# Multiplying s by c for two neighbouring units in one GpSimd operation, in a selective-scan and expert kernel

## The chip, the cores and the metric

The kernel runs on one core of a Trainium2 chip. The metric is the device time of one execution in microseconds (us). A core has five engines that run their own instruction streams and wait for each other at semaphores: TensorE (PE in the profile), VectorE (DVE), ScalarE (ACT), GpSimd (POOL) and SyncE (SP), which issues most of the DMA transfers. VectorE, ScalarE and TensorE's results share the eight banks of PSUM; GpSimd works on SBUF alone here.

## What is computed

The input is 32 sequences of 256 tokens with 128 features. Each token is normalised; the result is the input plus the output of a multi-head selective scan plus that of a mixture of 8 experts (top 1, with a capacity of 1024 tokens). The scan is what matters here:

```
def step(s, inp):
    d_t, u_t, B_t, C_t = inp
    dA = jnp.exp(d_t[..., None] * A)
    s = s * dA + (d_t * u_t)[..., None] * B_t[:, :, None, :]
    y_t = jnp.einsum('bhdn,bhn->bhd', s, C_t)
    return (s, y_t)
...
y = y + x * Dskip
y = y * jax.nn.silu(z)
out = y @ out_proj_w.T
```

There are 4 heads of 64 features, and 16 states n for each feature. All is in float32.

## The kernel before, in words

The 8192 tokens are cut into 16 chunks (0 to 15) of 512 tokens (two sequences). In a chunk the scan's 256 x 16 rows of state are cut into 32 units of 128 rows: unit w (0 to 31, `SLOTS`) holds 8 features with their 16 states. Units 0 to 15 are half 0, 16 to 31 half 1. All engines have a loop over w, and everything else is put into slots of this loop by hand-written tables (`STAGE_A`, `FFN`, `SOFTPLUS`, `GATE`, `GATHER`, `COMBINE`). The chunks run as: chunk 0; a loop over chunks 1 to 8, two in a pass, in which each chunk also computes one expert; a loop over chunks 9 to 14, two in a pass, in which the experts' rows are gathered back and added; chunk 15. The text calls 1 to 8 the second stage (FFN chunks) and 9 to 14 the third.

A unit goes through the engines like this:

- TensorE spreads d*u (L1182) and d (L1189) over the 128 rows into PSUM, two units ahead. The spread of d for unit w+2 waits for scan w-1; that of d*u waits for the u product before last of its bank.
- ScalarE takes the exponential of the spread d (L762).
- VectorE multiplies the spread d*u by B (L902, the u product; its order is u of unit w+1, then scan of unit w), and scans over time (L972) into `s_sb[:, w % 8, :]`, a ring of 8 buffers.
- GpSimd multiplies s by c in place (L578), `c_of[:, hf, hh, :]`, where `hh` changes every two units; it counts `p_ready`. In chunk 0 three of four of these products, in chunk 15 one of four, are made by VectorE (L979, `by_dve`), in chunks 1 to 14 none.
- TensorE sums the products of four units (a quad) over the states (L1204, `sum_quad`): quad k, units 4k to 4k+3, at w = 4k+6. The scan of unit 4k+8 overwrites the buffers and waits for that sum.

Around this, by slot w:

- TensorE and ScalarE also make the next chunk's inputs. ScalarE's silus of z and x (L675, L677, each pair between two table loads) stand at w = 9 and 19, TensorE's L1127 waits for them, and the output projection of the chunk before (L1147) stands at w = 9 and 10; VectorE's L872 adds its result at w = 11.
- VectorE, behind scan w: L860 at w = 5 and 21 (y plus D*x, one operand in PSUM), L864 at w = 6 and 22 (the gate, `g_sb` times `zs`, both in SBUF). In chunks 9 to 14 L893 at w = 14 to 21 (adds one gathered tile, `back` and `acc`, both in SBUF), the subtraction L908 (`split_low`, both in SBUF) at w = 7 and 24, and the small copy L886 at w = 0. In chunks 1 to 8 the small copy L992 at w = 16.
- GpSimd, behind product w: the scale L534 (`scale_x`, d times x) at w = 3 and 20; the memset L538 (`zero_first`) at w = 4 and 21, behind the product of its slot (the wait for the scale stands ahead of that product); in chunks 1 to 8 the subtraction L544 (`split_low`) at w = 7 and 24; in chunks 9 to 14 one indirect gather (L554) in each slot from 1 to 8. In chunk 0 it issues the 64 scatters L585.
- ScalarE rounds the result of the scale (L726, at w = 7 and 24) once the memset is done. The subtraction takes that, and its result is copied by four DMAs of SyncE (L434, `stack`) into `dsp`, which TensorE's spreads of the next half read. SyncE also loads `b_of` and `c_of` of a half (L446, `spread_bc`) once all products of the units that read the old ones are counted (`wait_products`).

Of the kernel before, what the change touches and what calls it, by code (L numbers as in the profile page):

```python
# [22 lines left out]
ALU = mybir.AluOpType  # L23
# [3 lines left out]
P = 128  # L27
# [5 lines left out]
CH = 512  # L33
CHUNKS = TOK // CH
# [4 lines left out]
UNITS = P // UC  # L39
SLOTS = HALVES * UNITS  # L40
QUADS = P // 32
U_RING, S_RING = 4, 2 * QUADS
# [44 lines left out]
def bass_mamba_moe(nc, hidden, in_w, conv_w, conv_b, xp_w, dt_w, dt_b, a_log, d_skip, out_w,  # L87
                   wg, w1, b1, w2, b2, consts, out):
    ctx = ExitStack()
    with ctx:  # L90
        def sb(name, shape, dt=F32):
            return ctx.enter_context(nc.sbuf_tensor(name, shape, dt))
# [58 lines left out]
        c_of = sb("c_of", [P, HALVES, 2, CH])  # L151
        u_sb = sb("u_sb", [P, U_RING, CH])
        s_sb = sb("s_sb", [P, S_RING, CH])
# [201 lines left out]
        def by_dve(ch, w):  # L355
            return w % QUADS < {0: HELP, CHUNKS - 1: HELP_LAST}.get(ch[0], 0)
# [148 lines left out]
        @block.gpsimd  # L505
        def _(pool):
            pool.memset(zero, 0.0).then_inc(S["zero_ready"], 1)
            pool.memset(xin, 0.0).then_inc(S["xin_zeroed"], 1)
            pool.memset(xnT[:, :, 0:TAPS - 1], 0.0).then_inc(S["xin_zeroed"], 1)
            pool.memset(weff[:, :, :], 0.0).then_inc(S["xin_zeroed"], 1)  # L510
            pool.memset(wg_sb[:, EXP:32], 0.0).then_inc(S["xin_zeroed"], 1)
            pool.memset(neg_m, -SP_M)
            pool.memset(neg_t, -SP_T)
            pool.memset(log_t1, LN_C1 - SP_M)
            pool.memset(log_t2, LN_C2 - 2 * SP_M)
            pool.memset(none, 0.0).then_inc(S["xin_zeroed"], 1)
            for b in (1, 3):
                pool.wait_ge(S["sp_chain"], 2 * b + 2)
                pool.wait_ge(S[f"x_loaded{b}"], 16)
                centre(pool, b).then_inc(S["centred_pool"], 1)  # L520
            for b in range(LN_BLK - 1):
                t = slice(b * BT, (b + 1) * BT)
                pool.wait_ge(S["rstd_ready"], b + 1)
                pool.tensor_tensor(xn[:, t, :], xn[:, t, :],
                                   rstd[:, t].unsqueeze(2).broadcast_to([P, BT, DM]),
                                   ALU.mult).then_inc(S["xn_ready"], 1)

            def scale_x(ch, hf):

                wait(pool, "stacked", per_chunk(ch, 128, 64 * hf))  # L530
                if ch == (0, None) and hf == 0:
                    pool.wait_ge(S["ein_zeroed"], 16 * EXP)
                pool.wait_ge(*tile_read(delta_in(ch, hf), f"D{hf}"))
                pool.tensor_tensor(dd[:, 1, :], dd[:, 0, :], xs_of(ch, hf), ALU.mult).then_inc(S["dx_ready"], 1)  # L534

            def zero_first():

                pool.memset(dd[:, 0, :].rearrange("p (s t) -> p s t", s=SEQS)[:, :, 0:1], 0.0  # L538
                            ).then_inc(S["dd_ready"], 1)

            def split_low(ch, hf):

                pool.wait_ge(S["hi_ready"], per_chunk(ch, 2, hf + 1))
                pool.tensor_tensor(lo, dd, hi.bitcast(F32), ALU.subtract).then_inc(S["lo_ready"], 1)  # L544

            scale_x((0, None), 0)
            pool.wait_ge(S["dx_ready"], 1)
            zero_first()
            split_low((0, None), 0)

            def gathers(tiles=range(GROUP)):

                for n in tiles:
                    pool.indirect_dma_start(back[:, n, :], None, eout[:, :],  # L554
                                            bass.IndirectOffsetOnAxis(ap=take_now[:, n:n + 1], axis=0),
                                            ).then_inc(S["back_loaded"], 16)

            def body(ch):
                for w in range(SLOTS):
                    hf, hh = w // UNITS, head_of(w)  # L560
                    if w == 1 and has_combine(ch):
                        pool.wait_ge(S["eo_free"], 16 + 32 * EXP)
                        pool.wait_ge(S["take_ready"], lin(ch, lambda c: c - FIRST_COMBINE + 1))

                    span = QUADS if ch[0] == 0 else 1
                    due = lambda what: [x for v in range(w - span + 1, w + 1) if w % span == span - 1
                                        for x in softplus_now(ch, v, what)]
                    zero_now = due("zero")
                    for of, hf_, _ in zero_now:
                        pool.wait_ge(S["dx_ready"], per_chunk(of, 2, hf_ + 1))  # L570
                    if not by_dve(ch, w):
                        if not any(by_dve(ch, v) is False for v in range(w // UNITS * UNITS, w)):
                            pool.wait_ge(*bc_loaded(ch, hf, "c"))
                        if w % UNITS == UNITS - 1 and ch[0] + 1 < CHUNKS:
                            pool.wait_ge(*tile_read(ch, f"bc{w // UNITS}"))
                        pool.wait_ge(S["scan_done"], per_chunk(ch, SLOTS, w + 1))
                        s_now = s_sb[:, w % S_RING, :]
                        pool.tensor_tensor(s_now, s_now, c_of[:, hf, hh, :], ALU.mult).then_inc(S["p_ready"], 1)  # L578
                    if zero_now:
                        zero_first()  # L580
                    if ch[0] == 0:
                        if w == 0:
                            pool.wait_ge(S["routed"], 2)
                        for i in range(w * TILES // SLOTS, (w + 1) * TILES // SLOTS):
                            pool.indirect_dma_start(ein[:, :],  # L585
                                                    bass.IndirectOffsetOnAxis(ap=put_at[:, i:i + 1], axis=0),
                                                    xn[:, i, :], None).then_inc(S["scattered"], 16)
                    for of, hf_, _ in softplus_now(ch, w, "scale"):
                        scale_x(of, hf_)
                    if low_by_pool(ch):  # L590
                        for of, hf_, _ in due("low"):
                            split_low(of, hf_)
                    if GATHER <= w < GATHER + GROUP and has_combine(ch):
                        gathers((w - GATHER,))
                    if ch[0] == CHUNKS - 1 and LAST_GATHER <= w < LAST_GATHER + GROUP:
                        if w == LAST_GATHER:
                            pool.wait_ge(S["take_ready"], TILES // GROUP)
                        gathers((w - LAST_GATHER,))

            chunks(pool, body, lambda: None)  # L600


# [705 lines left out]
```

## Time and profile before

| | |
|---|---|
| median of 3 runs | 1237.58 us (1233.49 to 1238.75) |
| profiled execution | 1234.84 us, span 1232.9 us |
| TensorE matmul busy | 1022.4 us (83%) |
| VectorE busy | 1070.5 us (87%) |
| ScalarE busy | 734.7 us (60%) |
| GpSimd busy | 858.9 us (70%) |
| products on GpSimd (L578) | 480, 628.5 us |
| mean granted TensorE clock | 0.901 of full speed |

The shares are means over the whole span. The views used below are: groups of instructions by shape, with the mean duration and the idle time before them; the waits, by who waited for whom; the chain of work that ended last, which is followed back from the last instruction; and the timeline, instruction by instruction. In the timeline a row is: start, duration, engine, line, operation, output and inputs, count, and in brackets the idle time of the engine before it with its releaser. The durations of two rows of VectorE overlap a little (a scan of 1.21 us is followed by the next operation after 1.13). A scan that ends is seen as the start of what VectorE does behind it.

### The profile page before, as it was taken

Reading aid. Unit: us, or ns where it says so; the run is one execution under the profiler, and the core shown is the slowest. Engines: PE = TensorE matmul, PEld = TensorE weight load, DVE = VectorE, ACT = ScalarE, POOL = GpSimd, SP = SyncE. Lnnn points to the kernel's source line nnn. Section 1 sums busy time; section 2 is a strip of 40 time slices with the busy share of each in tenths; the row PEclk is TensorE's granted clock in tenths of the full one; section 3 lists DMA queues with packets and bytes.
Section 4 is the critical chain, followed back from the end, with each engine's and each line's share of the span. In section 5 each row is a group of like instructions: output and inputs, shape, how many; then the busy total and the mean of one; then the engine's idle time right before and its main releaser. Section 6 shows DMA issues by size and latency. Waiting matters only on the chain.

```text
span 1232.9 us, 15308 instructions
## 1 busy us (share of the span) xinstructions
PE 1022.4 (83%) x3821; PEld 476.4 (39%) x3821; DVE 1070.5 (87%) x1331; ACT 734.7 (60%) x1117; POOL 858.9 (70%) x708
## 2 busy tenths in 40 slices
PE   0755858999999899999999997888888888888785
PEld 0522324444545454444445453333333333243322
DVE  7647968889898979899898989999898989999996
ACT  2564535767586776767685766556564756555421
POOL 2335788767676867677676769687777868686755
PEclk9988868999999999999999999788887979797765
DMA  6542325243432424342534423442434333343311
GB/s 160 157 94 68 91 79 130 57 99 69 107 80 64 103 62 111 77 94 51 119 68 98 89 57 80 86 86 48 87 71 90 81 73 68 82 85 80 72 36 34
DMA packets 81065, 103.01 MB, mean 84 GB/s; under 512 B 13280, under 2 KB 51072, under 8 KB 81024
## 3 DMA queue, kind: packets, MB, share of 16 engines
q1 hardware_dynamic: 76928, 94.18, 35.3%
q0 software_dynamic: 4096, 8.40, 2.3%
q8 instruction: 12, 0.20, 0.1%
q14 instruction: 29, 0.24, 0.1%
HBM read 18.66 MB, written 16.78 MB: 29 GB/s over the span
## 4 chain that ended last, share of the span: by engine, by line
PE 40%; DVE 24%; issue 22%; POOL 7%; ACT 3%; DVEq 1%; DMA 1%; SPq 1%; POOLq 0%; ACTq 0%
DVE u_sb L902 10%; DVE s_sb L972 8%; PE bank L1204 6%; PE bank L1171 5%; PE bank L1189 5%; PE bank L1127 4%; PE bank L1182 4%; PE bank L1114 3%; POOL expert_in L585 3%; PE bank L1135 2%; PE bank L1136 2%; PE bank L1137 2%; POOL s_sb L578 2%; PE bank L1147 2%; DVE g_sb L860 2%
## 5 line engine op out<-in xcount | busy, mean ns | idle before, releaser
L578 POOL TENSOR_TENSOR s_sb<-s_sb,c_of 128x512 f32<-128x512 f32 x480 | 628.5, 1315 | 273.2 <-DVE s_sb L972 265.1
L972 DVE TENSOR_TENSOR_SCAN s_sb<-bank,u_sb 128x512 f32<-128x512 f32 x512 | 620.4, 1212 | 0.0
L762 ACT ACTIVATE bank<-bank,a_neg 128x510 f32<-128x510 f32 x512 | 334.0, 659 | 255.9 <-PE bank L1189 246.4
L902 DVE TENSOR_TENSOR u_sb<-bank,b_of 128x512 f32<-128x512 f32 x512 | 346.2, 676 | 98.7 <-PE bank L1182 94.9
L1182 PE MATMUL bank<-dsp,sel_d 128*128 128x512 f32 x512 | 316.1, 617 | 39.8 <-DVE u_sb L902 20.4
L1189 PE MATMUL bank<-dsp,sel_d 128*128 128x512 f32 x512 | 244.5, 478 | 79.0 <-DVE s_sb L972 71.5
L1182 PEld LDWEIGHTS bank<-dsp,sel_d 128*128 128x128 f32 x512 | 104.6, 204 | 243.4 <-DVE u_sb L902 147.6
L1189 PEld LDWEIGHTS bank<-dsp,sel_d 128*128 128x128 f32 x512 | 106.5, 208 | 195.4 <-DVE s_sb L972 163.0
L1204 PE MATMUL bank<-s_sb,con 128*32 128x512 f32 x1024 | 161.2, 706 | 12.7 <-POOL s_sb L578 6.8
L1114 PE MATMUL bank<-xnT,wx 128*128 (+1 forms) x256 | 128.8, 597 | 0.0
L585 POOL DMA_INDIRECT expert_in<-xn,put_at x64 | 65.6, 1026 | 17.9 <-issue 17.8
L554 POOL DMA_INDIRECT xn<-expert_out,take_now x64 | 66.0, 1031 | 10.5 <-issue 7.4
L726 ACT ACTIVATE hi<-dd 128x1024 fp32r<-128x1024 f32 x32 | 33.9, 1058 | 61.8 <-POOL dd L538 61.8
L1127 PE MATMUL bank<-xs,bcw 128*64 128x512 f32 x64 | 46.7, 822 | 27.5 <-ACT xs L677 27.5
L1171 PE MATMUL bank<-xn 128*128 128x128 f32 x512 | 64.0, 278 | 6.4 <-ACT xn L737 6.4
L1171 PEld LDWEIGHTS bank<-xn 128*128 128x128 f32 x512 | 60.7, 191 | 17.3 <-ACT xn L737 9.9
L534 POOL TENSOR_TENSOR dd<-dd,xs 128x512 f32<-128x512 f32 x32 | 40.9, 1277 | 34.2 <-ACT dd L720 34.1
L1164 PE MATMUL bank<-xn 128*128 128x512 f32 x128 | 64.4, 605 | 0.3
L1114 PEld LDWEIGHTS bank<-xnT,wx 128*128 128x128 f32 x256 | 47.4, 189 | 27.7 <-issue 22.8
L720 ACT ACTIVATE dd<-bank,small 128x512 f32<-128x512 f32 x32 | 22.1, 690 | 52.6 <-PE bank L1138 51.6
L737 ACT ACTIVATE xn<-bank,b_now 128x512 f32<-128x512 f32 x64 | 43.1, 688 | 14.5 <-PE bank L1164 13.9
L1204 PEld LDWEIGHTS bank<-s_sb,con 128*32 128x32 f32 x1024 | 21.4, 114 | 60.0 <-issue 44.9
(140 smaller groups left out, 1045.0 us busy)
## 6 DMA issues: line engine op xcount, KB each, us to landing
b_of<-bc SPq DMA_DIRECT2D x64, 256.0 KB
c_of<-bc SPq DMA_DIRECT2D x64, 256.0 KB
dsp<-hi SPq DMA_DIRECT2D x64, 256.0 KB
dsp<-dd SPq DMA_DIRECT2D x64, 256.0 KB
expert_in<-dd SPq DMA_DIRECT2D x8, 512.0 KB, 6.4
xn<-expert_in SPq DMA_DIRECT2D x8, 512.0 KB, 5.4
xn<-L_ffn_W SPq DMA_DIRECT2D x16, 256.0 KB, 4.6
expert_out<-xn SPq DMA_DIRECT2D x16, 256.0 KB, 2.4
```

The lines of the kernel that those rows point to most:

```text
L554: pool.indirect_dma_start(back[:, n, :], None, eout[:, :], bass.IndirectOffsetOnAxis(ap=take_now[:, n:n + 1], axis=0),).then_inc(S["back_l ...
L578: pool.tensor_tensor(s_now, s_now, c_of[:, hf, hh, :], ALU.mult).then_inc(S["p_ready"], 1)
L585: pool.indirect_dma_start(ein[:, :], bass.IndirectOffsetOnAxis(ap=put_at[:, i:i + 1], axis=0), xn[:, i, :], None).then_inc(S["scattered"], 16)
L762: act.activation(d, d, ACT.Exp, scale=a_neg[:, k:k + 1]).then_inc(S["decay_ready"], 1)
L902: dve.tensor_tensor(u_sb[:, w % U_RING, :], du_ps[w % 2][:, :], b_of[:, hf, head_of(w), :], ALU.mult).then_inc(S["u_ready"], 1)
L972: dve.tensor_tensor_scan(s_sb[:, w % S_RING, :], decay_of(w)[:, :], u_sb[:, w % U_RING, :], 0.0, ALU.mult, ALU.add).then_inc(S["scan_done" ...
L1114: mm = pe.matmul(t[:, :], wx[:, hf, part, :], xnT[:, seqs, part:part + SEQ], start=(part == 0), stop=(part == TAPS - 1))
L1127: pe.matmul(t[0:4 * NS, :] if name[0] == "b" else t[:, :], w[:, hf, :], xs_of(ch, hf), start=True, stop=True).then_inc(S["misc_pe"], 1)
L1171: mm = pe.matmul(t[:, part * P:(part + 1) * P], hT[:, f, part * P:(part + 1) * P], w2_sb[:, f, :], start=(f == 0), stop=(f == FT - 1))
L1182: pe.matmul(du_ps[w % 2][:, :], sel_d[:, group_of(w), :, :].rearrange("k n d -> k (n d)"), dsp[:, hf, head_of(w), 1, :], start=True, stop= ...
L1189: pe.matmul(decay_of(w)[:, :], sel_d[:, group_of(w), :, :].rearrange("k n d -> k (n d)"), dsp[:, w // UNITS, head_of(w), 0, :], start=True ...
L1204: mm = pe.matmul(y_ps[q * 32:(q + 1) * 32, :], con[:, K_SUM + 32 * r:K_SUM + 32 * (r + 1)], s_sb[:, (QUADS * k + q) % S_RING, :], start=(r ...
```

## The change

In chunks 1 to 14 GpSimd makes the products of units w-1 and w (w odd) in one operation of 2 x 512 elements. At even w it makes none. It waits for scan w, and adds 2 to `p_ready`. The second operand is the same row of `c_of` for both units, repeated by a stride of zero (`broadcast_to`). Chunks 0 and 15 keep one product for each unit. The same lines set `span` to 2 in these chunks. `span` decides where the memset L538 (`due("zero")`) and GpSimd's subtraction L544 (`due("low")`) stand: what was due at w-1 or w is made at odd w. So the memset of w = 4 is made at w = 5, behind the pair (4,5), and the subtraction of w = 24 at w = 25, behind the pair (24,25). Those of w = 21 and 7 stay. The scales (w = 3 and 20) and the gathers (w = 1 to 8) stay in their slots.

```
-                    span = QUADS if ch[0] == 0 else 1
+                    two = 0 < ch[0] < CHUNKS - 1
+                    span = QUADS if ch[0] == 0 else 2 if two else 1
                     due = lambda what: [x for v in range(w - span + 1, w + 1) if w % span == span - 1
                                         for x in softplus_now(ch, v, what)]
...
-                    if not by_dve(ch, w):
-                        if not any(by_dve(ch, v) is False for v in range(w // UNITS * UNITS, w)):
+                    if not by_dve(ch, w) and (w % 2 or not two):
+                        if not any(by_dve(ch, v) is False for v in range(w // UNITS * UNITS, w - two)):
                             pool.wait_ge(*bc_loaded(ch, hf, "c"))
                         if w % UNITS == UNITS - 1 and ch[0] + 1 < CHUNKS:
                             pool.wait_ge(*tile_read(ch, f"bc{w // UNITS}"))
                         pool.wait_ge(S["scan_done"], per_chunk(ch, SLOTS, w + 1))
-                        s_now = s_sb[:, w % S_RING, :]
-                        pool.tensor_tensor(s_now, s_now, c_of[:, hf, hh, :], ALU.mult).then_inc(S["p_ready"], 1)
+                        n = 2 if two else 1
+                        s_now = s_sb[:, w % S_RING + 1 - n:w % S_RING + 1, :]
+                        pool.tensor_tensor(s_now, s_now, c_of[:, hf, hh, :].unsqueeze(1).broadcast_to([P, n, CH]),
+                                           ALU.mult).then_inc(S["p_ready"], n)
```

## Rows read from the trace of the kernel before

**Rows 1.** Chain that ended last, 909:977 us: start us, us, engine and line.

```profile
957.66 0.06 ACT bank L762
...
973.96 0.33 DVE acc L893
```

**Rows 2.** Waits of the whole run: who waited for whom, total us, times, longest.

```profile
ACT hi L726 <- POOL dd L538: 61.8, 32, 14.7
```

**Rows 3.** Groups by shape, GpSimd: xcount | busy us, mean ns | idle us before, releasers.

```profile
L578 POOL TENSOR_TENSOR s_sb<-s_sb,c_of 128x512 f32<-128x512 f32 x480 | 628.5, 1315 | 273.2 <-DVE s_sb L972 265.1 <-POOL dd L534 3.5 <-DMA expert_out<-xn 1.0
...
L544 POOL TENSOR_TENSOR dd<-dd,hi 128x1024 fp32r<-128x1024 f32 x17 | 40.1, 2358 | 1.2 <-ACT hi L726 1.2
...
L524 POOL TENSOR_TENSOR xn<-xn,sp_x 128x2048 f32<-128x2048 f32 x3 | 10.8, 3609 | 6.4 <-DVE sp_x L825 6.4
```

**Rows 4.** Timeline, chunk 12, units 1 to 8: start us, us, engine, operation [idle before].

```profile
946.74 1.29 POOL L578 TENSOR_TENSOR s_sb<-s_sb,c_of 128x512 f32<-128x512 f32 x1 [0.51 <-DVE s_sb L972]
...
948.18 1.00 POOL L554 DMA_INDIRECT xn<-expert_out,take_now  x1
...
956.55 0.12 POOL L538 MEMSET dd<- 128x2 f32 x1
...
956.70 1.06 ACT L726 ACTIVATE hi<-dd 128x1024 fp32r<-128x1024 f32 x1 [2.46 <-POOL dd L538]
...
958.90 1.28 ACT L675 ACT_TABLE_LOAD   x1
...
961.42 1.97 PE L1127 MATMUL bank<-xs,bcw 128*64 128x512 f32 x2 [1.49 <-ACT xs L677]
```

**Rows 5.** Timeline, chunk 4, units 4 to 11: GpSimd, ScalarE, VectorE.

```profile
406.57 0.10 POOL L538 MEMSET dd<- 128x2 f32 x1
...
406.70 1.06 ACT L726 ACTIVATE hi<-dd 128x1024 fp32r<-128x1024 f32 x1 [0.72 <-POOL dd L538]
...
410.08 1.28 ACT L675 ACT_TABLE_LOAD   x1
...
408.74 0.67 DVE L864 TENSOR_TENSOR g_sb<-g_sb,zs 128x512 f32<-128x512 f32 x1
...
417.96 0.69 DVE L872 TENSOR_TENSOR acc<-bank,acc 128x512 f32 x1
```

**Rows 6.** Timeline, chunk 15: a product and a VectorE operation beside it.

```profile
1161.99 1.28 POOL L578 TENSOR_TENSOR s_sb<-s_sb,c_of 128x512 f32<-128x512 f32 x1
...
1162.16 1.67 DVE L864 TENSOR_TENSOR g_sb<-g_sb,zs 128x512 f32<-128x512 f32 x1
```

**Rows 7.** Timeline, chunk 9: a run of products and a VectorE operation beside it.

```profile
761.92 7.44 POOL L578 TENSOR_TENSOR s_sb<-s_sb,c_of 128x512 f32<-128x512 f32 x6
...
766.44 3.07 DVE L893 SCALAR_TENSOR_TENSOR acc<-xn,gate,acc 128x128 f32 x1
```

**Rows 8.** Timeline, chunk 12, units 14 and 15: VectorE and GpSimd.

```profile
973.96 0.33 DVE L893 SCALAR_TENSOR_TENSOR acc<-xn,gate,acc 128x128 f32 x1
...
974.12 1.30 POOL L578 TENSOR_TENSOR s_sb<-s_sb,c_of 128x512 f32<-128x512 f32 x1 [0.15 <-DVE s_sb L972]
...
975.94 0.33 DVE L893 SCALAR_TENSOR_TENSOR acc<-xn,gate,acc 128x128 f32 x1
```

**Rows 9.** Timeline, chunk 11, units 19 to 21: VectorE, then GpSimd.

```profile
915.58 0.33 DVE L893 SCALAR_TENSOR_TENSOR acc<-xn,gate,acc 128x128 f32 x1
...
916.75 0.69 DVE L902 TENSOR_TENSOR u_sb<-bank,b_of 128x512 f32<-128x512 f32 x1 [0.84 <-PE bank L1182]
...
918.49 0.33 DVE L893 SCALAR_TENSOR_TENSOR acc<-xn,gate,acc 128x128 f32 x1
...
920.46 0.72 DVE L860 SCALAR_TENSOR_TENSOR g_sb<-xs,small,bank 128x512 f32<-128x512 f32 x1
...
921.10 0.34 DVE L893 SCALAR_TENSOR_TENSOR acc<-xn,gate,acc 128x128 f32 x1
...
919.92 1.26 POOL L534 TENSOR_TENSOR dd<-dd,xs 128x512 f32<-128x512 f32 x1
```

## The prediction, made before the changed kernel was run

> **What bounds the kernel now.** I read first the chain of work that ended last over one chunk of the third stage (chunks 9 to 14, some 68 us each). From scan 6 it goes over ScalarE (957.66), which must finish the silu of x before TensorE can go on, and comes back to VectorE for units 11 to 16 (973.96 is one of its pieces) [rows 1]. The other pieces are VectorE's and TensorE's in turn. The reader is to see that GpSimd's products are not in it: a faster product by itself shortens nothing. Then the totals of the waits: one GpSimd result is waited for in every half of a chunk, the small memset L538, by ScalarE's rounding L726, 61.8 us in 32 waits [rows 2]. ScalarE works through its list in order, so what is late there pushes the exponentials and the silus behind it. Last the timeline around the places where GpSimd and VectorE meet.
>
> **What one operation costs.** A product of 512 elements takes 1315 ns on average. The nearest row to the new operation is L544, two inputs of 1024 elements: 2358 ns. L524 has 2048 elements, one input repeating a single value along a row: 3609 ns, 1.76 ns an element, so 1.80 us for 1024, some 1.90 with a start cost [rows 3]. The new operand repeats a whole row of 512 and not one value, so I take 2.36 us, with the bounds 1.90 and 2.63 (two products). Over 14 chunks that is 224 x 0.27 = 61 us less work for GpSimd. I cost this gain at nothing, since by the first paragraph no product is in the chain.
>
> **The moved memset, third stage.** The diff changes `span` to 2 as well. So the memset due at w = 4 is made at w = 5, and there it stands behind the pair (4,5). Now the order from w = 1 is product 1, gather, product 2, gather, product 3, scale, gather, product 4, memset: 946.74 to 956.55 [rows 4]. New: pair (0,1), two gathers, pair (2,3), scale, two gathers, pair (4,5), memset. A product followed by a gather takes 1.44 (946.74 to 948.18), a gather some 1.0 to 1.3 [rows 4]; a pair takes 1.04 us more than a product. The scan of unit 1 is awaited by both, and the pairs (2,3) and (4,5) find their scans done. Pair and gap 2.54, gathers 1.3 + 1.0, pair 2.32, scale and gap 1.44, gathers 1.3 + 1.0, pair 2.32: 13.3 instead of 9.8. The memset comes at 960.0, 3.45 late.
>
> Who waits: L726 starts 0.15 behind the memset today (956.70, after 2.46 us idle), then two exponentials, then the table load of the silu at 958.90, then TensorE's L1127 at 961.42, which already idles 1.49 for it [rows 4]. No slack: all four move by 3.45, and 957.66 and 961.42 are pieces of the chain [rows 1]. TensorE has the spreads of the next units queued behind L1127, so VectorE follows. VectorE's subtraction L908 at w = 7 also waits for L726; that delay lies within this one. 3.4 us a chunk, 20.4 for six. If the pair costs 1.90, three pairs are 1.4 shorter: 2.05 a chunk.
>
> **The same in the second stage (chunks 1 to 8).** Memset at 406.57, L726 at 406.70 (idle 0.72), the table load of the silu at 410.08 [rows 5]. New: the scale ends at about 406.3, the pair (4,5) begins at 406.5, the memset at 408.85, L726 ends at 410.05, two exponentials, table load at 411.2: 1.1 late. TensorE's projections and its output product are queued behind it, and VectorE's L872, at 417.96 with no idle time to speak of [rows 5], waits for the latter. So 1.1 us a chunk, 8.8 for eight. At 1.90 it is 0.65.
>
> **The port.** Some VectorE operations can't run beside a GpSimd product. L864 (both inputs in SBUF) takes 0.67 us at 408.74 [rows 5]. The one issued at 1162.16, behind a product begun at 1161.99, took 1.67 and ended 0.56 after the product's end at 1163.27, so it began 0.1 before that [rows 6]. In chunk 9 an L893, which normally takes 0.33, took 3.07: six products ran without a gap from 761.92 to 769.36, and it ended at 769.51 [rows 7]. L860, with one operand in PSUM, took 0.72 beside the scale of 919.92 [rows 9], so it is free of this.
>
> Now these meetings are rare because of the order: the product starts 0.16 us behind VectorE's L893 (973.96, 974.12) and ends before the next one, at 975.94 [rows 8]. With pairs this breaks at every even unit: the pair (w-1, w) starts behind scan w and lasts 2.36, and VectorE reaches the operations behind scan w+1 after 1.98 us, or 1.7 without an L893 between. In the third stage:
> - w = 14: the port is free 2.34 behind scan 13, L893 comes at 1.71: 0.6 us, in a VectorE part of the chain [rows 1].
> - w = 16, 18: free at 2.44, L893 at 1.98: 0.46 each. VectorE now idles 0.84 before the u product at 916.75 [rows 9], which takes up all but 0.1.
> - w = 20: the pair (18,19) begins 0.16 behind L893 of unit 19 (915.58) and ends 2.54 behind it; the scale L534 now follows without a gap, as no product of unit 20 stands before it, and ends 1.22 later. L893 of unit 20 (918.49, with the shifts so far some 2.1 behind that of 19) gets in only behind the scale: 1.56.
> - w = 21: L860 (920.46) stands between scan 21 and L893 (921.10) [rows 9]. The pair (20,21) begins 0.1 behind the scan, L893 comes at 0.64: 2.46 - 0.64 - 0.1 = 1.7.
> - w = 6, 7, 22, 24: L864 and L908. Units 6, 7 and 22 find GpSimd idle or gathering by then, and at 24 the chain has gone to TensorE. At nothing; without that cover up to 0.7 each.
>
> Sum 0.6 + 0.1 + 1.56 + 1.7 = 4.0 a chunk, 24 for six, less 2.7 for the long wait of chunk 9, which the later and gapped pairs there end: 21.3. In the second stage there is no L893; L864 at w = 6 and 22 comes 2.37 behind a scan, a pair ends at 2.5: 0.15 each, 2.4 in all. The small copy L992 at w = 16 may meet the port too, but the chain is on TensorE by then: nothing.
>
> **Other moves, all at nothing.** The subtraction L544 at w = 24 of the second stage moves to 25 and behind a pair, some 2.7 us later; SyncE's four copies of its result are due at TensorE's w = 30. At w = 7 it is 1.1 later, like everything there. If these copies are missed, 1 us a chunk, 8 in all. TensorE's sum of a quad is issued two units behind its last product, about 3.4 us, and the product ends 1.1 later. The loads of b and c shift by 1.1 and are due a half later.
>
> **Sum.** The profiled execution took 1234.84 us (span 1232.9), 2.7 under the median. 20.4 + 8.8 + 21.3 + 2.4 = 53: 1288.
>
> **A rule against the trace.** The Trainium skill (SBUF — State Buffer, Who interferes with whom) says that a VectorE instruction with two SBUF inputs and a GpSimd one that reads SBUF exclude each other, and whoever starts first holds the port for the whole instruction. The 1.67 us row agrees. By this rule the port is free at each instruction's end, while the 3.07 us row has VectorE shut out over two such ends. It is the second rival below.
>
> **The rivals.**
> - *Memset only (0.13).* VectorE's waits at the port fall into its idle times before TensorE. 29 + 3: 1267 us. For it: VectorE idles in each chunk. Against it: w = 14 is in the chain.
> - *Free at every end (0.10).* w = 20 then waits 0.34 instead of 1.56, so 7 us less: 1281.
> - *A cheap pair (0.10).* At 1.90: 2.05 x 6 + 0.65 x 8 = 17.5 for the memset; of the port w = 14 costs 0.2, 20 and 21 1.2 each, 2.6 a chunk, 15.6 less 2.7. Sum 30: 1265. Only L524 speaks for it.
> - *A dear pair (0.05).* At 2.63 the memset costs 0.8 a third-stage chunk more, the port 1.1, a second-stage chunk 0.5: 15 more, 1303. TensorE's granted clock might fall in the new idle time and add to this.
> - *Absorbed (0.07).* ScalarE and TensorE make up for the late memset within the chunk, and the port is as in the first rival: 1238, no change. Against it speaks that L1127 idles for ScalarE already.
> - *Faster (0.05).* The place is the same memset, the point is GpSimd's time from w = 1 to it. If a pair cost under about 1.2 us, hardly more than one product, the memset would come no later than now, the 2.7 of chunk 9 would go and at w = 21 it would come up to 0.6 earlier in six chunks: 6.4 less, 1228. Against it speak all rows for 1024 elements and more.
>
> **How the numbers follow.** The forecast of 1288 has 0.50; its own range is 1276 to 1302. About 0.5% (6 us) is what a measurement of this kernel can tell from no change. Slower: 0.50 + 0.13 + 0.10 + 0.10 + 0.05 = 0.88; no change 0.07, faster 0.05. For 8 in 10 the range leaves out the last two and the far end of the dear pair: 1255 to 1304.
>
> **What would show it.** The pair at about 2.36 us, 224 times, and GpSimd's busy time down by 60. ScalarE's wait for the memset (L726) up from 61.8 by some 30 to 40 us; TensorE's L1127 waiting 3 us and more for ScalarE in chunks 9 to 14. L893 long at 14, 16, 18, 20 and 21, normal at 15, 17 and 19. A third-stage chunk at 75 us instead of 68, a second-stage one at 69.5. Chunks of 72 with a short L893 would be the memset alone; L893 at 1.7 us and an unchanged L726 would refute the first half, a pair at 1.9 the price.

## The result, and the profile after

The changed kernel took 1292.92 us (median, 1291.93 to 1294.15), the kernel before 1235.69 beside it: ratio 1.047, 95% interval 1.045 to 1.049, slower. The forecast was 1288, with a range of 1255 to 1304. The profiled execution of after has a span of 1292.2 us, 59.3 more than that of before. From the product on, lines of the new kernel stand two or three further down: the product is L580, the rounding L729, the gate product L867, the combine L896, the subtraction L911, the projection L1130.

First the groups by shape that answer to [rows 2, 3] (columns as in [rows 3]):

```profile
L580 POOL TENSOR_TENSOR s_sb<-s_sb,c_of 128x1024 f32<-128x1024 f32 x224 | 533.8, 2383 | 350.9 <-DVE s_sb L975 350.2 <-POOL dd L534 0.2
...
L1130 PE MATMUL bank<-xs,bcw 128*64 128x512 f32 x64 | 47.5, 834 | 41.6 <-ACT xs L680 41.6
...
L867 DVE TENSOR_TENSOR g_sb<-g_sb,zs 128x512 f32<-128x512 f32 x32 | 37.6, 1174 | 0.0
...
L896 DVE SCALAR_TENSOR_TENSOR acc<-xn,gate,acc 128x128 f32 x48 | 36.8, 766 | 0.0
...
L729 ACT ACTIVATE hi<-dd 128x1024 fp32r<-128x1024 f32 x32 | 33.8, 1057 | 105.0 <-POOL dd L538 105.0
...
L911 DVE TENSOR_TENSOR dd<-dd,hi 128x1024 fp32r<-128x1024 f32 x15 | 23.0, 1531 | 16.7 <-ACT hi L729 16.7
```

The pair takes 2383 ns, 224 times. GpSimd works 51 us less (858.9 to 807.8 us), and nobody gains: in its new idle time it waits for scans. What has grown are others' rows: ScalarE's wait for the memset from 61.8 [rows 2] to 105.0, TensorE's for the silu of x from 27.5 to 41.6, the gate product from a mean of 737 to 1174 ns, the combine from 385 to 766, the subtraction from 1269 to 1531. The page shows VectorE busy 44 us longer (1070.5 to 1114.5) with the same work: time at a shut port counts as busy.

Scan 0 of a chunk to scan 0 of the next gives the time by stage:

| chunks | before, us | after, us | more |
|---|---|---|---|
| 0 | 91.4 | 92.3 | +0.9 |
| 1 to 8 | 551.9 | 571.5 | +19.6 |
| 9 to 14 | 412.0 | 452.1 | +40.1 |

A third-stage chunk takes 75.1 to 76.0 instead of 68.2 or 68.3 (chunk 9: 70.7). In the second stage most take 71.2 or 71.3 instead of 68.1, but chunk 6 only 69.6, and chunk 2 takes 69.6 in both kernels. In chunk 2 of before the granted clock had already fallen once (to its lower level at units 8 to 10), which it did not in chunk 2 of after.

**Chunk 12, slot by slot.** I laid the scans of chunk 12 of both kernels over each other; the lateness grows behind these units: 6 by 2.8 us, 9 to 11 by 0.7, 14 by 0.7, 16 and 18 by 0.4 each (0.6 of it given back at 19), 20 by 0.2, 21 by 1.7, 24 by 0.8. In all 6.9. The timeline around unit 6, GpSimd, then VectorE, ScalarE and TensorE:

```profile
995.30 0.94 POOL L554 DMA_INDIRECT xn<-expert_out,take_now  x1 [0.30 <-issue]
996.26 2.36 POOL L580 TENSOR_TENSOR s_sb<-s_sb,c_of 128x1024 f32<-128x1024 f32 x1
998.54 0.12 POOL L538 MEMSET dd<- 128x2 f32 x1
...
995.76 3.42 DVE L867 TENSOR_TENSOR g_sb<-g_sb,zs 128x512 f32<-128x512 f32 x1
...
1000.83 1.19 DVE L911 TENSOR_TENSOR dd<-dd,hi 128x1024 fp32r<-128x1024 f32 x1
...
998.70 1.06 ACT L729 ACTIVATE hi<-dd 128x1024 fp32r<-128x1024 f32 x1 [5.68 <-POOL dd L538]
...
1000.89 1.28 ACT L678 ACT_TABLE_LOAD   x1
...
1003.41 1.97 PE L1130 MATMUL bank<-xs,bcw 128*64 128x512 f32 x2 [1.65 <-ACT xs L680]
```

The memset comes 16.2 us after scan 0, before it was 12.9 [rows 4]; the 3.35 late go on to the table load unchanged. But VectorE stands too: the gate product, issued 0.46 us into a gather, ends 0.5 us after the pair behind that gather, after 3.42 us instead of 0.67. TensorE therefore idles 1.65 for the silu, hardly more than the 1.49 of [rows 4]: both are late together. Chunk 9 is the exception: there the gate product took 0.67 us, and the chunk was late all the same, by 4.6 us up to unit 12. The combines of chunk 12:

```profile
1016.11 1.06 DVE L896 SCALAR_TENSOR_TENSOR acc<-xn,gate,acc 128x128 f32 x1
...
1018.82 0.32 DVE L896 SCALAR_TENSOR_TENSOR acc<-xn,gate,acc 128x128 f32 x1
...
1020.79 0.76 DVE L896 SCALAR_TENSOR_TENSOR acc<-xn,gate,acc 128x128 f32 x1
...
1025.19 0.76 DVE L896 SCALAR_TENSOR_TENSOR acc<-xn,gate,acc 128x128 f32 x1
...
1029.86 0.49 DVE L896 SCALAR_TENSOR_TENSOR acc<-xn,gate,acc 128x128 f32 x1
1032.64 2.09 DVE L896 SCALAR_TENSOR_TENSOR acc<-xn,gate,acc 128x128 f32 x1
```

Long at 14, 16, 18 and 21, somewhat long at 20, 0.32 at 15, 17 and 19: the pattern that was foreseen, but for the size at 20.

**Chunks 4 and 6.** In both the table load is 1.15 us later than before (1.1 was forecast), and L1130 idles 1.96 us in place of 0.92. Then they part. TensorE's rows of chunk 4, then of chunk 6, and the stretches with the granted clock (the number ahead of the last two):

```profile
418.65 1.07 PE L1130 MATMUL bank<-xs,bcw 128*64 128x512 f32 x2 [1.96 <-ACT xs L680]
...
420.59 1.91 PE L1150 MATMUL bank<-wzo,g_sb 128*128 128x128 f32 x8
...
561.14 1.07 PE L1130 MATMUL bank<-xs,bcw 128*64 128x512 f32 x2 [1.96 <-ACT xs L680]
...
562.72 1.05 PE L1150 MATMUL bank<-wzo,g_sb 128*128 128x128 f32 x8
...
418.00:422.00 4.00, 3.35 (x11) 2.35 (x12) 3.16 (x4) 3.58 (x6) 4.00 (x3) 0.72 0.00 0
422.00:426.00 4.00, 4.00 (x24) 2.35 (x23) 2.46 (x4) 0.74 (x2) 2.33 (x2) 0.85 0.97 216
...
560.00:564.00 4.00, 2.86 (x14) 1.76 (x14) 3.37 (x5) 3.97 (x6) 4.00 (x3) 1.00 0.00 0
564.00:568.00 4.00, 4.00 (x25) 2.34 (x24) 3.72 (x6) 1.73 (x4) 3.42 (x2) 1.00 0.85 189
```

After the same idle time the clock stays at the upper of its two levels (2.4 GHz) in chunk 6 and falls to the lower (1.2 GHz) in chunk 4 (0.72 and 0.85 are means over both levels). The units 9 to 11 lose 1.0 us in chunk 6 and 2.6 in chunk 4.

### The profile page after: what moved, and what is told of

Read it like the earlier page. It is cut to its first block, busy times and chain, and to the rows that moved or that the text cites. A ratio compares the mean times of both kernels' runs of the same rounds, so it can differ in the third digit from the quotient of the medians.

```text
span 1292.2 us, 15073 instructions
## 1 busy us (share of the span) xinstructions
PE 1035.7 (80%) x3821; PEld 483.0 (37%) x3821; DVE 1114.5 (86%) x1331; ACT 733.7 (57%) x1117; POOL 807.8 (63%) x484
## 3 DMA queue, kind: packets, MB, share of 16 engines
q1 hardware_dynamic: 76928, 94.18, 33.8%
## 4 chain that ended last, share of the span: by engine, by line
PE 39%; DVE 25%; issue 22%; ACT 6%; POOL 5%; DVEq 1%; DMA 1%; SPq 1%; ACTq 0%; POOLq 0%
DVE u_sb L905 9%; PE bank L1207 6%; DVE s_sb L975 6%; PE bank L1174 5%; PE bank L1192 4%; PE bank L1130 4%; PE bank L1185 4%; PE bank L1150 3%; DVE g_sb L867 3%; PE bank L1138 2%; POOL expert_in L588 2%; PE bank L1117 2%; PE bank L1139 2%; PE bank L1140 2%; DVE g_sb L863 2%
## 5 line engine op out<-in xcount | busy, mean ns | idle before, releaser
L580 POOL TENSOR_TENSOR s_sb<-s_sb,c_of 128x1024 f32<-128x1024 f32 (+1 forms) x256 | 577.1, 2255 | 380.9 <-DVE s_sb L975 379.9
L1207 PE MATMUL bank<-s_sb,con 128*32 128x512 f32 x1024 | 156.2, 685 | 13.3 <-POOL s_sb L580 9.1
L729 ACT ACTIVATE hi<-dd 128x1024 fp32r<-128x1024 f32 x32 | 33.8, 1057 | 105.0 <-POOL dd L538 105.0
L1130 PE MATMUL bank<-xs,bcw 128*64 128x512 f32 x64 | 47.5, 834 | 41.6 <-ACT xs L680 41.6
L1174 PEld LDWEIGHTS bank<-xn 128*128 128x128 f32 x512 | 60.7, 192 | 17.3 <-ACT xn L740 9.9
L1150 PEld LDWEIGHTS bank<-wzo,g_sb 128*128 128x128 f32 x256 | 43.0, 245 | 19.2 <-issue 16.7
```

Source lines behind the costliest of these rows:

```text
L580: pool.tensor_tensor(s_now, s_now, c_of[:, hf, hh, :].unsqueeze(1).broadcast_to([P, n, CH]), ALU.mult).then_inc(S["p_ready"], n)
L1130: pe.matmul(t[0:4 * NS, :] if name[0] == "b" else t[:, :], w[:, hf, :], xs_of(ch, hf), start=True, stop=True).then_inc(S["misc_pe"], 1)
L1150: mm = pe.matmul(t[:, i * P:(i + 1) * P], g_sb[:, hf, i * P:(i + 1) * P], wo[:, hf, :], start=(hf == 0), stop=(hf == HALVES - 1))
L1174: mm = pe.matmul(t[:, part * P:(part + 1) * P], hT[:, f, part * P:(part + 1) * P], w2_sb[:, f, :], start=(f == 0), stop=(f == FT - 1))
L1207: mm = pe.matmul(y_ps[q * 32:(q + 1) * 32, :], con[:, K_SUM + 32 * r:K_SUM + 32 * (r + 1)], s_sb[:, (QUADS * k + q) % S_RING, :], start=(r ...
```

## Experiments

All ratios are to the kernel before, measured beside each run (1234.6 to 1237.2 us). Times by stage are those of the profiled executions. "Places" below means the units at which the scans of a chunk fall behind.

**1. The two halves of the change apart.** `memset_back` has pairs, and the memset at w = 4 as before, as a subtraction of a small tile from itself:

```diff
-                    span = QUADS if ch[0] == 0 else 2 if two else 1
+                    span = QUADS if ch[0] == 0 else 1
...
-                    if zero_now:
+                    if zero_now and two and w % 2 == 0:
+                        z = dd[:, 0, :].rearrange("p (s t) -> p s t", s=SEQS)[:, :, 0:1]
+                        pool.tensor_tensor(z, z, z, ALU.subtract).then_inc(S["dd_ready"], 1)
+                    elif zero_now:
```

> The changed kernel with the pairs kept, but the clearing of the first column and the second stage's subtraction back at w = 4 and 24 (span as in the kernel before; the clearing at w = 4 is a tiny tensor_tensor, z - z, in place of the memset, since it now carries a wait). Theory M (the late memset is the main cost in both stages): back come 3.4 us in each of chunks 9 to 14 and 2.6 or 1.0 in chunks 1 to 8, about 38 us: 1255. Theory P (in the third stage the wait of L867 for the port at w = 6, 2.8 us, covers the late memset and stays without it): the third stage gives back only 0.7 a chunk, the second the same as under M: about 22 us, 1271.

Measured: 1275.17 us, ratio 1.031 [1.027, 1.035]. `span_only` is the kernel before with the new span alone and single products:

```diff
-                    span = QUADS if ch[0] == 0 else 1
+                    two = 0 < ch[0] < CHUNKS - 1
+                    span = QUADS if ch[0] == 0 else 2 if two else 1
```

> The kernel before with the move of the memset to w = 5 (behind the single product of unit 5) and of the subtraction to w = 25, and nothing else: no pairs. Theory M: the memset is 2.4 us late in the third stage, with no slack behind it, so 14 us for six chunks; in the second stage it is 1.3 late, of which 0.2 reach the path: 1252 against 1236. Theory P (a late memset costs only because pairs shut VectorE out): within 3 us of the kernel before, 1238.

Measured: 1253.57 us, ratio 1.014 [1.010, 1.017]. Against the kernel before beside them (1237.23) the two halves cost 37.9 and 16.3 us, 54.3 against 57.2 for both together. That is nearly a sum, but by stage it is none. Chunks 1 to 8 lose 3.3 us with pairs alone, 0.1 with the late memset alone and 19.6 with both. There the memset of `span_only` comes 1.2 us late and the table load not at all; only pair and span together use up ScalarE's slack, and then the clock falls more often (experiment 3). In chunks 9 to 14 the pairs alone lose 35.8 us of the 40.1 (1.9 in chunk 9 against 5.2, 33.8 against 34.8 in the other five): with the memset in time, the gate product still stands at the port. Chunk 12 of `memset_back`, GpSimd, then VectorE, then ScalarE:

```profile
976.07 0.96 POOL L554 DMA_INDIRECT xn<-expert_out,take_now  x1 [0.15 <-issue]
977.05 2.36 POOL L580 TENSOR_TENSOR s_sb<-s_sb,c_of 128x1024 f32<-128x1024 f32 x1
...
976.94 3.03 DVE L870 TENSOR_TENSOR g_sb<-g_sb,zs 128x512 f32<-128x512 f32 x1
...
980.07 1.28 ACT L681 ACT_TABLE_LOAD   x1 [1.79 <-DVE g_sb L870]
```

ScalarE's silu overwrites what the gate product reads, so its table load now waits 1.79 us for the gate product and comes 17.3 us after scan 0: 2.1 later than before, with the memset in time.

The small gain from the timely memset hides something. In chunk 12 `memset_back` gains 1.9 us on after at units 6 and 9 to 11, and loses as much again at units 27, 31 and 1. Around those units TensorE's granted clock stays longer at its lower level: over the whole chunk 27.3 us, against 20.5 in after and 20.4 in before. Why it does was not tested.

The late memset alone (`span_only`) costs some 3 us a third-stage chunk, at units 1, 7 and 9 to 11, with 1.3 given back at 27: the subtraction at w = 7 waits 0.85 us for ScalarE, and comes 0.97 us into a gather:

```profile
968.09 1.00 POOL L554 DMA_INDIRECT xn<-expert_out,take_now  x1 [0.16 <-issue]
969.10 1.28 POOL L579 TENSOR_TENSOR s_sb<-s_sb,c_of 128x512 f32<-128x512 f32 x1
...
969.06 2.41 DVE L909 TENSOR_TENSOR dd<-dd,hi 128x1024 fp32r<-128x1024 f32 x1 [0.85 <-ACT hi L727]
```

So either half alone brings VectorE to a shut port near unit 6 or 7 and makes ScalarE late, and with both the two delays run side by side.

**2. The combines at the port.** `odd_combine` is the kernel after with the combines of chunks 9 to 14 behind odd scans:

```diff
-                        if COMBINE <= w < COMBINE + GROUP:
-                            ins = combine(ch, w - COMBINE)
+                        at = [15, 17, 19, 23, 25, 27, 29, 31] if ch[0] < CHUNKS - 1 else list(range(COMBINE, COMBINE + GROUP))
+                        if w in at:
+                            ins = combine(ch, at.index(w))
...
```

> The changed kernel with VectorE's combining operations (L896) in chunks 9 to 14 moved from units 14 to 21 to 15, 17, 19, 23, 25, 27, 29 and 31, behind whose scans VectorE comes before the pair. Theory P: the waits for the port at 14, 16, 18, 20 and 21 go, which the slots of the trace put at 2.9 us a chunk on the path: 17 us, 1276. Theory M: these waits were idle time of VectorE anyway: 1293, unchanged.

Measured: 1276.8 us, ratio 1.033 [1.029, 1.036]. The group's mean over all 64 combines falls from 688 to 352 ns, chunks 9 to 14 take 436.2 us instead of 452.1, and a chunk 72.1 to 73.3: the combines are worth 16 us. In chunks 11 and 14 the gate product took only 0.67 us, and yet they were 4.8 us late by unit 12, where chunks 10 and 13, with a gate product of 3.4 and 3.5 us, were 3.5 us late: with the memset late, a free port for the gate product saved nothing.

**3. The granted clock.** `dummy_mm` adds two matmuls, whose result nobody reads, ahead of the waiting L1130 in chunks 1 to 14:

```diff
+                    for _ in range(2 if src[0] >= 1 else 0):
+                        pe.matmul(t[0:4 * NS, :], bcw[:, hf, :], wx[:, hf, :, :].rearrange("p k m -> p (k m)"),
+                                  start=True, stop=True)
```

> The changed kernel with two matmuls whose result is overwritten, put on TensorE ahead of its wait for ScalarE's silu (L1130), in chunks 1 to 14. They do work of no use, about 1.7 us of it, in the time in which TensorE idled. Theory C (in six of the eight chunks 1 to 8 TensorE's granted clock falls to half after this idle time, and that costs 1.6 us each): the clock stays at 1.0 there, these chunks take 69.6 instead of 71.3, about 10 us less: 1283. Theory W (only the wait for ScalarE counts; the clock after it has no cost): 1293 or a little more, since the added matmuls are late themselves.

Measured: 1333.73 us, ratio 1.078 [1.075, 1.082], which neither theory foresaw. The reason is in two rows of chunk 4:

```profile
424.81 3.03 PE L1129 MATMUL bank<-wx,bcw 128*64 128x512 f32 x4 [1.39 <-ACT zs L678]
427.63 1.67 PE L1133 MATMUL bank<-xs,bcw 128*64 128x512 f32 x2
```

The extra matmuls write the bank that ScalarE's silu of z must read first, so they themselves waited 1.39 us and delayed the real ones. In chunks 2, 4, 6 and 8 the clock fell all the same; in 3, 5 and 7 it stayed up, and they still took 72.6 us. This says nothing on the cause of the fall. What the runs show is a count over chunks 2 to 8 of the other twelve kernels. Where L1130 (or its line in that kernel) idled 1.95 to 2.69 us, the clock fell to its lower level at units 8 to 11 in 27 of 42 chunks (after, `no_repeat`, `odd_combine`: 5 of 7 each; `gate7`, `gate7_memset_back`, `all_odd`: 4 of 7 each). Where it idled 0.79 to 0.93 us, the clock fell somewhere in 8 of 42 (one or two in each of before, `span_only`, `gather5`, `early_pairs`, `odd_memset`, `memset_back`). So most falls go with the longer idle time, but a late memset is not needed for one. Why chunk 6 of after escapes with the same 1.96 us stays open.

**4. Moving the gate out of the way.** `gate7` is the kernel after with one number changed, which puts the second gate product at w = 7 and 23; `gate7_memset_back` does it on `memset_back`:

```diff
-GATE = (5, 6)
+GATE = (5, 7)
```

> The changed kernel with VectorE's gate product L867 one unit later, at w = 7 and 23 in place of 6 and 22. Its 2.8 us wait for the port at w = 6 in chunks 9 to 14 goes. Theory O (the late memset and this wait lie beside each other, each alone costs about 3 us a chunk and both together 3.5): the memset then shows in full, behind ScalarE's silu, and the third stage stays within 0.7 us a chunk of the changed kernel: 1289 to 1294. Theory P alone (the wait at w = 6 is the cost): 2.8 us a chunk come back, 1276.

> Both edits: the gate product at w = 7 and 23, and the clearing at w = 4 again (as the z - z operation) with the subtraction at 24. Pairs kept. Theory O: only now the first part of the third-stage chunk is free; against memset_back (1275) some 2.2 us a chunk come back, since the gate product still waits 0.7 at w = 7: 1262. If the two costs were simply added, memset_back would have shown the memset's share already, and this run would give 1275 less 2.8 x 6 = 1258; if the wait at w = 6 is harmless, 1275.

Measured: 1288.19 us, ratio 1.045 [1.042, 1.047], and 1279.88 us, ratio 1.037 [1.035, 1.040]. The first bears out theory O: in chunk 12 the gate product takes 1.24 us instead of 3.42,

```profile
992.56 1.24 DVE L867 TENSOR_TENSOR g_sb<-g_sb,zs 128x512 f32<-128x512 f32 x1
```

and the chunk still takes 75.1 us. Its 2.8 us at unit 6 are gone and come back at units 7 and 9 to 11, behind the late memset: TensorE now idles 4.84 us for the silu instead of 1.65. The second is 5 us slower than `memset_back`, against every theory: it wins 4.6 us in chunks 9 to 14 and loses 11.6 in chunks 1 to 8. Chunk 4 of it, ScalarE, then TensorE:

```profile
414.78 1.28 ACT L681 ACT_TABLE_LOAD   x1 [1.14 <-DVE g_sb L870]
...
417.30 1.17 PE L1133 MATMUL bank<-xs,bcw 128*64 128x512 f32 x2 [2.64 <-ACT xs L683]
...
419.42 1.91 PE L1153 MATMUL bank<-wzo,g_sb 128*128 128x128 f32 x8
```

ScalarE's silu overwrites the zs that the gate product reads. Gate product one unit later, table load later, TensorE idles 2.64 us, and L1153 runs at 1.91 us instead of 1.05: the clock has fallen again, as in chunks 2, 5 and 7; in 3, 6 and 8 it did not. I had looked only at the port. With the memset late the move cost nothing in these chunks (567.3 us in `gate7` against 571.5 in after), as the table load was late already.

**5. All at once, with that mistake and without.** `all_odd` is `gate7_memset_back` with the combines of experiment 2 and the small copy of b one unit earlier; `odd_memset` is the same with the gate back at 6:

```diff
-            b1_slot = FFN["xt0"][0] - 2
+            b1_slot = FFN["xt0"][0] - 3
```

> gate7_memset_back with VectorE's combining operations at 15, 17, 19, 23, 25, 27, 29, 31 (chunks 9 to 14) and the small copy at w = 15: pairs everywhere, but every VectorE operation with a port conflict behind an odd scan, except the subtraction at w = 24. If the port and the memset are the whole cost of the change, little is left of it: 1262 less 17 and less 3 is 1242, within 1% of the kernel before. If the pairs cost by their later products (sums, loads of b and c), 1255 or more.

> The kernel after with three edits: the small clearing at w = 4 again, the eight combines at w = 15, 17, 19, 23, 25, 27, 29, 31 in chunks 9 to 14, and the small copy of b one unit earlier, at w = 15. The gate stays at w = 5 and 6. Places theory (each wait is paid at its own place, and taking one away leaves the others as they are): from the 1275.2 us with the clearing back, some 2.8 us go in each of the six third-stage chunks (the long combines at 14, 16, 18, 20, 21) and some 0.4 in each of the eight of the second stage (the copy): 1255 us, within 4; a third-stage chunk at 72.2 us, a second-stage one at 68.1 to 68.2. What is left in a third-stage chunk then stands at w = 6 (the gate) and w = 24 (the subtraction). Takeover theory (the time saved at one place is lost at the next meeting, as when the gate was moved): a third-stage chunk stays at 74 or more, 1268 us.

Measured: 1268.92 us, ratio 1.028 [1.026, 1.030], and 1245.14 us, ratio 1.008 [1.005, 1.010]. The first missed its forecast through the moved gate: 563.3 us in chunks 1 to 8, and in chunk 12 a combine of 2.42 us at w = 23, where the gate product now stood ahead of it and pushed it beside the next pair. The second is 10 us better than its own forecast. Chunks 1 to 8 are back at 552.5 (0.6 over before), chunks 9 to 14 at 419.3 (7.3 over). Moving the combines was worth 28 us here (447.8 to 419.3) and 16 in experiment 2. In chunk 13, beside the 3.7 us at units 14 to 21, over 1 us more goes at unit 27, so the places do not simply add. The clock goes with it: in chunk 13 it is at its lower level for 15.9 us, against 27.3 in `memset_back`. How much of the 28 us is the clock's was not separated. In chunks 9, 12 and 14 the gate product even found the port open, as these rows of chunk 12 and then chunk 13 of `odd_memset` show:

```profile
961.33 0.67 DVE L870 TENSOR_TENSOR g_sb<-g_sb,zs 128x512 f32<-128x512 f32 x1
...
963.64 2.66 DVE L914 TENSOR_TENSOR dd<-dd,hi 128x1024 fp32r<-128x1024 f32 x1
...
1030.74 0.96 POOL L554 DMA_INDIRECT xn<-expert_out,take_now  x1 [0.15 <-issue]
1031.72 2.36 POOL L580 TENSOR_TENSOR s_sb<-s_sb,c_of 128x1024 f32<-128x1024 f32 x1
...
1031.61 3.03 DVE L870 TENSOR_TENSOR g_sb<-g_sb,zs 128x512 f32<-128x512 f32 x1
```

Where the gate product passes, the subtraction behind it pays (2.66 instead of 1.2), but the chunk takes 69.0 us instead of 70.8. Which of the two happens goes with the clock at the chunk's start: in chunks 10, 11 and 13 it is at its lower level up to 1.5 to 2.2 us behind scan 0, and scan 2 comes 0.9 to 1.3 us later than in chunks 12 and 14, where it is at its upper level by scan 0.

**6. Other gather times.** `gather5` is the kernel before with its gathers four units later (`GATHER` 5 instead of 1), which frees GpSimd around the memset.

> The kernel before (single products) with the eight gathers of chunks 9 to 14 at w = 5 to 12 in place of 1 to 8. Then three gathers fewer stand ahead of the memset of w = 4, which comes 1.9 us earlier, and TensorE's L1127 (idle 1.5 for ScalarE) with it. If the memset's place in GpSimd's queue costs the kernel before something too, this is faster: VectorE idles 0.7 a chunk there, so 4 us, 1232. Against it: the gathers then meet the gate product and the subtraction at w = 6 and 7, and the products of 9 to 13 run back to back into the combining operation of w = 14 (3 us in chunk 9 now, if in all six chunks 15 us more): 1250.

Measured: 1259.67 us, ratio 1.022 [1.019, 1.025]. In chunk 12 the memset came 12.1 us behind scan 0 instead of 12.9 (1.9 earlier was forecast) and L1127 idled 0.93 us instead of 1.49, but the combine at w = 14 now waits 2.98 us for gathered rows:

```profile
987.76 0.98 DVE L893 SCALAR_TENSOR_TENSOR acc<-xn,gate,acc 128x128 f32 x1 [2.98 <-DMA xn<-expert_out,take_now]
```

VectorE's idle time before the combines is 22.0 us in this run, against 2.4 in before. The gathers' place in the kernel before has a reason that I had not priced.

**7. Pairs where nothing meets them.** `early_pairs` has pairs in chunks 1 to 8 alone, with the memset at w = 4 and the copy at w = 15:

```diff
-                    two = 0 < ch[0] < CHUNKS - 1
+                    two = 0 < ch[0] < FIRST_COMBINE
...
```

> Pairs in chunks 1 to 8 alone, with the small clearing at w = 4 and the copy of b at w = 15 (one unit earlier, in all chunks); chunks 9 to 14 have single products as before. Places theory: nothing that VectorE, ScalarE or TensorE waits for is later than before in these chunks but the gate product at w = 6 and 22, 0.12 us each, and GpSimd's 30 us less work bring nothing, since no product is in the chain: 68.1 to 68.3 us a chunk, 1234 to 1240 us, ratio 1.000 to 1.003. Load theory (GpSimd's fewer operations also take load off the rest: fewer meetings, fewer waits for products): second-stage chunks below 68.0 and a ratio under 0.997. Clock theory (a pair alone is enough to make TensorE's granted clock fall there): several chunks at 69.6, 1243 us or more.

Measured: 1238.39 us, ratio 1.0016 [1.0003, 1.0029]: 128 pairs, with every meeting taken away but the 0.12 us of each gate product, bring nothing. Chunks 3 to 8 take 68.3 to 68.5 where the clock stays up; in chunk 5 it fell at units 15 and 16, which cost 1.6 us more by unit 19. No variant with pairs beat the kernel before.

**8. The repeated row.** `no_repeat` multiplies by two neighbouring rows of c instead of one row twice:

```diff
-                        pool.tensor_tensor(s_now, s_now, c_of[:, hf, hh, :].unsqueeze(1).broadcast_to([P, n, CH]),
+                        pool.tensor_tensor(s_now, s_now, c_of[:, hf, hh:hh + 1, :] if n == 1 else c_of[:, hf, :, :],
```

> The kernel after, with one change in what is computed: in a pair the second factor is not the same row of c for both units but two neighbouring rows, 1024 different elements without a repeat; so the products of one unit of each pair are made with the wrong row, and nothing else changes. If the repeated row costs GpSimd extra, the pair falls well below 2383 ns, to 2100 or less, and the kernel gets some us faster through earlier ends of the port waits. If it costs nothing to speak of, the pair stays within 40 ns of 2383 (the existing operation of this size takes 2358) and the kernel at 1291 to 1294 us.

Measured: 1294.55 us in one run, and the L580 group (256 operations of both sizes) at a mean of 2257 ns against 2255 in after; the pairs alone at 2385 against 2383. The repeat is free: 1024 different elements take as long.

## Why the prediction held, and where its steps did not

- **The bound, and GpSimd's saving at nothing: right.** `early_pairs` shows it for chunks 1 to 8. For chunks 9 to 14 no run frees the pairs of every meeting; that no variant with pairs was faster there agrees with it. The saving itself was 51 us, not 61, in the main because two products of these chunks took 2.62 us and the pair 2.38, a difference of 0.24 and not 0.27.
- **The pair at 2.36 us: right** (2.383). The nearest row, L544, was the right one [rows 3]; experiment 8 shows that the repeat adds nothing.
- **The memset 3.45 late in the third stage: right as a time (3.35; its terms add up to 13.2, not 13.3), and right in the sum by luck.** The step that failed was "Units 6, 7 and 22 find GpSimd idle or gathering by then", "At nothing": at unit 6, with a pair ready behind the gather, the gate product waits 2.4 to 2.8 us in chunks 10 to 14. The forecast's 3.4 a chunk is the measured lateness by unit 12 (3.5 in chunk 12), but the scans fall behind at unit 6 by the gate product's wait (2.8) and only by 0.7 more behind the memset. The missed wait did not add to the sum, because it runs side by side with the memset's delay. Taking away either alone frees next to nothing: without the late memset (`memset_back`) five chunks together gain 1 us, without the gate product's long wait (`gate7`) they gain 0.8 us. Where both are away, in chunks 12 and 14 of `odd_memset`, the scans are only 0.8 and 0.4 us late by unit 12, helped by the clock at the chunk's start (experiment 5). The term that was forecast for the memset was the price of the two together.
- **The memset in the second stage: right in the mechanism (table load 1.15 late, 1.1 forecast), mis-sized in the sum.** The term was 1.1 a chunk. It measured 1.0 where the clock stayed up and 2.6 where it fell. The clock fall stood only as an addition to the dear pair. Of the 8.4 us by which 19.6 exceeds the forecast 11.2 it makes most: 8 us in chunks 3, 4, 5, 7 and 8, less the 1.6 of chunk 2, where it had fallen before the change and not after. The small copy (below) makes about 3, and the gate products at w = 6 and 22 cost 0.12 each against 0.15 forecast.
- **w = 14, 16, 18, 21: right.** Extra 0.73, 0.44, 0.44 and 1.77 against 0.6, 0.46, 0.46 and 1.7; 0.6 given back at 19, as forecast by VectorE's idle time. The end of chunk 9's long wait gives 2.0 back, against 2.7.
- **w = 20: wrong.** 1.56 forecast, 0.17 measured. The scale followed the pair without a gap (1027.82 + 2.38, then 1030.15), yet the combine issued at 1029.86 took 0.49 and was through by 1030.35. The forecast had taken the 3.07 us row of [rows 7] as the rule: VectorE shut out as long as GpSimd's operations follow without a gap. By the Trainium skill (SBUF — State Buffer, Who interferes with whom) whoever issues first has the pair of ports that VectorE and GpSimd share for the whole instruction. By that a waiting VectorE operation would get in at the next end; the row of 0.49 us agrees with this, the row of 3.07 us does not. What tells the two apart no run here shows.
- **w = 24: 0.8 a chunk that was put at nothing.** That "at 24 the chain has gone to TensorE" was wrong for the kernel after: its subtraction at w = 24 (1.95 us instead of 1.20) is a piece of the chain that ended last.
- **The small copy at w = 16: 0.90 us instead of 0.14 at the port**; of 0.77 lost VectorE's idle time gives 0.4 back. In `odd_memset`, with the copy one unit earlier, it takes 0.14 again. It was put at nothing.
- **The third stage in all:** 41.7 forecast, 40.1 measured; the second 11.2 against 19.6; chunk 0 and the start 0 against -0.4. The sum of 53 became 59.3. The total came close by luck as well: the wait at w = 6 hid beside the memset's delay, w = 24 stood in for part of w = 20, and what the third stage fell short of was outweighed by the clock in the second.

Of the rivals, "memset only" fell with the combines of 1.06 and 2.09 us, "a cheap pair", "a dear pair" and "faster" with the pair of 2383 ns, "absorbed" with the 7 us a third-stage chunk. Of "a dear pair" its last sentence came true, that the clock might fall in the new idle time. "Free at every end" had w = 20 right (0.34 forecast, 0.17 measured), but its 1281 needed the rest unchanged.

## What to carry over

An engine that is off the chain can still set the pace by when it holds a shared port and when it delivers a small by-product: before making its operations longer, list every operation of the bounding engine that needs the same port, with its offset to the long one, and every small result that stands behind it in the queue. A meeting costs up to a whole long operation, and whether it happens can change with a microsecond of lateness. Two delays that run side by side cost once, so a sum can come out right with one of them missing; only taking each away by itself shows it. When moving an operation away from a collision, look first for who waits for its end: with the memset in time the gate product moved by one unit cost 11.6 us in eight chunks.

## What the hardware showed that I had not expected

**The port seems taken before the product's row begins.** A gate product issued behind a gather whose next product is ready: issued 0.26 us after the gather's start it took 0.67 (`odd_combine`, chunk 11), 0.35 after it 3.52 (`odd_combine`, chunk 13), 0.46 after it 3.42 and 0.87 after it 3.03 (chunk 12 of after and of `memset_back`). The long ones all end 0.5 us or so after the pair's end. Where the product had to wait for a scan that ended only then, VectorE won: in after the subtraction at 1000.83, 0.48 us into a gather, took 1.19, and the pair behind it 2.92 instead of 2.36. So a gather itself does not shut VectorE out; a ready pair behind it seems to, from up to 0.6 us before its own row starts. A small ready operation did not: in chunk 9 of `memset_back` and of `odd_memset`, where the subtraction of 128x2 that replaces the memset stood behind the gather, the gate product was issued 0.90 and 0.59 us into it and took 0.67, and the small one took 0.62 and 0.31 instead of 0.21. This is read from rows of four kernels; no kernel was made to test it alone.

**A copy with one input, of 4 values a lane, waits too.** The copy of 128x4 took 0.90 us beside a pair (0.14 before).

**The clock can fall or not after equal idle times** (1.96 us ahead of L1130 in chunks 4 and 6), and a fall costs 1.6 us in a chunk of the second stage, in part in the eight matmuls L1150 (1.91 against 1.05 us), the rest in what stands behind them.
